# Row sums of a causal attention: partial sums of probability tiles made by adding DMAs in place of GpSimd additions, and a new layout of these tiles

## The reference

```python
q = (x @ wq).reshape(4, 512, 32, 32)
k = (x @ wk).reshape(4, 512, 8, 32)         # each key head serves 4 query heads
v = (x @ wv).reshape(4, 512, 8, 32)
q, k = rope(q), rope(k)
scores = q . k / sqrt(32), causal
attn = softmax(scores)                      # here: exp(score - row max) / row sum
x = layernorm(x + (attn @ v) @ wo)
hidden = silu(x @ (gate_t * gate_s).T) * (x @ (up_t * up_s).T)   # 3584 wide
out = layernorm(x + hidden @ (down_t * down_s).T)
```

## Time and profile before

| | us |
|---|---|
| median of 2 runs | 1869.38 (1867.28 to 1871.48) |
| the profiled execution, its time | 1868.12 |
| its span in the trace | 1866.4 |
| PE busy in it | 1807.0 (97%) |
| DVE, ACT, POOL busy in it | 1187.7, 710.5, 543.6 |

### The profile page before, as it was taken

One profiled execution on the slowest core, in us unless ns is written; L12 is line 12 of the kernel. 1 busy time (PEld: TensorE's weight loads), 2 busy tenths in 40 slices (PEclk: granted clock), 3 DMA queues, 4 the chain that ended last, 5 costly groups with the idle time before them and its releaser, 6 DMA issues.

```text
span 1866.4 us, 27364 instructions
## 1 busy us (share of the span) xinstructions
PE 1807.0 (97%) x10528; PEld 882.0 (47%) x10528; DVE 1187.7 (64%) x2047; ACT 710.5 (38%) x1112; POOL 543.6 (29%) x845
## 2 busy tenths in 40 slices
PE   7889999999999998999999999999999999999997
PEld 4545655555555543444444444444444444444443
DVE  7877778668768764445544444745656765667645
ACT  5443444444434444436433343342232322222221
POOL 1354546456546564131000000211321211112103
PEclk9999999999999999999999999999999999999999
DMA  8543234334334398557644353649321211232301
GB/s 246 118 103 78 54 85 125 83 80 116 90 52 114 81 212 221 209 208 263 236 171 150 107 195 126 215 148 211 127 66 53 79 66 51 72 104 85 107 12 79
DMA packets 228162, 233.13 MB, mean 125 GB/s; under 512 B 183872, under 2 KB 184128, under 8 KB 228032
## 3 DMA queue, kind: packets, MB, share of 16 engines
q1 hardware_dynamic: 227168, 230.99, 42.2%
q10 hardware_dynamic: 864, 0.39, 0.1%
HBM read 122.55 MB, written 72.88 MB: 105 GB/s over the span
## 4 chain that ended last, share of the span: by engine, by line
PE 85%; DVE 6%; issue 3%; SPq 2%; POOL 2%; ACT 1%; DMA 1%; ACTq 0%; DVEq 0%; POOLq 0%
PE bank L1053 31%; PE bank L948 20%; PE bank L1074 13%; PE bank L1087 6%; PE bank L998 4%; PE bank L960 3%; PE bank L984 3%; PE bank L1013 2%; SPq L1587 2%; DVE down_forms L1391 1%; PE bank L963 1%; DVE gate_blocks L1385 1%; POOL p_tiles L1451 1%; DVE row_max L1267 0%; DVE up_blocks L1375 0%
## 5 line engine op out<-in xcount | busy, mean ns | idle before, releaser
L1053 PE MATMUL bank<-x_forms,weight_forms 128*128 128x512 f16 x3136 | 700.9, 379 | 12.7 <-DVE gate_blocks L1375 4.4
L1053 PEld LDWEIGHTS bank<-x_forms,weight_forms 128*128 128x128 f16 x3136 | 305.3, 98 | 387.0 <-DVE gate_blocks L1375 7.1
L1139 ACT ACTIVATE p_tiles<-bank 128x512 f32<-128x512 f32 (+1 forms) x352 | 193.0, 556 | 276.6 <-PE bank L984 273.5
L1267 DVE TENSOR_REDUCE row_max<-bank 128x1 f32<-128x384 f32 (+3 forms) x352 | 220.0, 636 | 98.2 <-PE bank L963 96.6
L1074 PE MATMUL bank<-down_forms 128*128 128x512 f16 x1152 | 259.6, 381 | 2.4 <-issue 2.4
L948 PE MATMUL bank<-wq_parts,xT_parts 128*128 128x256 f16 x1536 | 219.4, 275 | 8.9 <-DVE wq_parts L1231 8.7
L1410 DVE TENSOR_TENSOR acc<-bank,acc 128x512 f32<-128x512 f32 x188 | 127.6, 687 | 124.2 <-PE bank L1074 64.7
L1443 POOL TENSOR_SCALAR_AFFINE_SELECT p_tiles<-p_tiles 128x128 f32<-128x128 f32 (+2 forms) x352 | 139.0, 403 | 212.2 <-ACT p_tiles L1139 210.9
L1074 PEld LDWEIGHTS bank<-down_forms 128*128 128x128 f16 x1152 | 113.0, 98 | 139.7 <-issue 4.9
L948 PEld LDWEIGHTS bank<-wq_parts,xT_parts 128*128 128x128 f16 x1536 | 144.1, 98 | 56.8 <-issue 14.2
L948 PE MATMUL bank<-wo_parts,att_parts 128*128 128x512 f16 x672 | 170.1, 382 | 0.6 <-DMA att_parts<-att_spill 0.6
(11 more groups left out here) (114 smaller groups left out, 1999.9 us busy)
## 6 DMA issues: line engine op xcount, KB each, us to landing
weight_forms_spill<-weight_forms SPq DMA_DIRECT2D x28, 896.0 KB, 5.7
weight_forms<-weight_forms_spill SPq DMA_DIRECT2D x28, 896.0 KB, 4.5
x_forms_spill<-x_parts SPq DMA_DIRECT2D x56, 256.0 KB, 2.4
w_page<-gateT SPq DMA_DIRECT2D x28, 512.0 KB, 5.0
w_page<-upT SPq DMA_DIRECT2D x28, 512.0 KB, 4.0
w_page<-downT SPq DMA_DIRECT2D x28, 512.0 KB, 4.3
att_spill<-att_made SPq DMA_DIRECT2D x64, 128.0 KB, 2.1
down_forms<-x_spill SPq DMA_DIRECT2D x16, 512.0 KB, 3.4
```

What stands on the lines that cost most here:

```text
L1053: t = nc.tensor.matmul(strassen[bank_set(use)][to][:, :], w_form[:, use % 4, A_FORMS[a_form], k * P:(k + 1) * P], xF[:, :, B_FORMS[b_form] ...
L1139: nc.scalar.activation(p32[j][:, h0:h0 + heads, :], bank[5 + m % 2][:, 0:heads * n].rearrange("p (h c) -> p h c", c=n), ACT.Exp, scale=SCO ...
L1267: nc.vector.tensor_reduce(mx[:, u % 2, i, h0:h0 + ROW_HEADS[i]], bank[3 + m % 2][:, 0:ROW_HEADS[i] * n].rearrange("p (h c) -> p h c", c=n) ...
```

## The change

- `presum` is gone. In its place stands `fold`: a DMA issued by POOL that adds (`accum_op`) tile j + 1 into the queries that tile j shares with it, for j = 2, 1 and 0. Each fold waits for the `pv` of tile j and, for j < 2, until the fold before it has landed. These waits are on POOL, which runs in order.
- `sums` of the groups 0 to 28 takes tile 0 alone, since fold 0 has put everything into it. Groups 29 and 30 take two tiles and have the folds 2 and 1; the last one takes all four, as before.
- The next group's `exp` of tile j waits for the landing of fold j - 1 (j = 1, 2, 3), or for `sums` (j = 0).
- A tile is laid out by blocks of 128 queries, then heads, in place of heads, then queries. So what a fold adds is one contiguous run on each partition: 1536, 1024 and 512 numbers for folds 0, 1 and 2, or 768, 512 and 256 KB in all.
- The planner's figures: 1.2 us of POOL for a fold, 5.0 us until it lands, `sums` 7 ranks behind the last key scores in place of 3.5.

```diff
+EARLY = NU * UG - 3
+FOLD_ISSUE, FOLD_LANDS = 1.2, 5.0
+def summed(q):
+    return 1 if q < EARLY else 2 if q < NU * UG - 1 else NT
@@
-        freed = [("pv", *last, j), ("sums", *last) if j < 2 else ("presum", *last, j - 1)] if q else []
+        freed = [("pv", *last, j), ("sums", *last) if j < summed(q - 1) else ("fold", *last, j - 1)] if q else []
@@
-        if j in (1, 2) and not final:
-            put(PO, at + 4, .2 + REP * (S - (j + 1) * P) / 410, "presum", u, G, j,
-                after=[("pv", u, G, j)] + [("presum", u, G, 2)] * (j == 1))
+        if j < NT - 1 and j + 1 >= summed(q):
+            put(PO, at + 3.5, FOLD_ISSUE, "fold", u, G, j, after=[("pv", u, G, j)] + [("fold", u, G, j + 1)] * (j < NT - 2), lands=FOLD_LANDS)
@@
-        put(PE, at + 3.5, 3.0 if final else 1.5, "sums", u, G, takes="T", after=[("causal", *one)] + [("presum", u, G, 1)] * (not final))
+        put(PE, at + (7 if q < EARLY else 3.5), (.9, 1.6, 2.2, 2.5)[summed(q) - 1], "sums", u, G, takes="T", after=[("causal", *one)] + (
+            [("fold", u, G, summed(q) - 1)] if not final else []))
@@
-        p32 = [p_all[:, p_starts[j]:p_starts[j + 1]].rearrange("p (h c) -> p h c", h=REP) for j in range(NT)]
+        p32 = [p_all[:, p_starts[j]:p_starts[j + 1]].rearrange("p (i h c) -> p i h c", h=REP, c=P) for j in range(NT)]
@@ matmuls of pv and sums
-  value, p32[j][:, h, :]
+  value, p32[j][:, :, h, :]
@@ sums, on PE
-                    tiles = 2
-                    if u * UG + G == NU * UG - 1:
-                        tiles = NT
-                    else:
-                        on.wait_ge(s_pre, 2 * (u * UG + G + 1))
+                    q = u * UG + G
+                    tiles = summed(q)
+                    if tiles < NT:
+                        on.wait_ge(s_fold[tiles - 1], 16 * (q + 1))
@@ exp, on ACT
-                    if j < 2:
+                    if j < summed(q - 1):
                         on.wait_ge(s_sums, q)
                     else:
-                        on.wait_ge(s_pre, 2 * q - (j - 2))
-                    nc.scalar.activation(p32[j][:, h0:h0 + heads, :], bank[5 + m % 2][:, 0:heads * n].rearrange(
-                        "p (h c) -> p h c", c=n), ACT.Exp, scale=SCORE_DOWN).then_inc(s_exp, 1)
+                        on.wait_ge(s_fold[j - 1], 16 * q)
+                    nc.scalar.activation(p32[j][:, :, h0:h0 + heads, :], bank[5 + m % 2][:, 0:heads * n].rearrange(
+                        "p (h i c) -> p i h c", h=heads, c=P), ACT.Exp, scale=SCORE_DOWN).then_inc(s_exp, 1)
@@ on POOL
-                elif kind == "presum":
+                elif kind == "fold":
                     u, G, j = which
                     q = u * UG + G
                     on.wait_ge(s_pv, NT * q + NT - j)
-                    on.wait_ge(s_pre, 2 * q + 2 - j)
-                    to = p32[j][:, :, P:S - j * P]
-                    nc.gpsimd.tensor_tensor(to, to, p32[j + 1][:, :, :], ALU.add).then_inc(s_pre, 1)
+                    if j < NT - 2:
+                        on.wait_ge(s_fold[j + 1], 16 * (q + 1))
+                    to, more = (t.rearrange("p i h c -> p (i h c)") for t in (p32[j][:, 1:NT - j, :, :], p32[j + 1][:, :, :, :]))
+                    e.dma_start(to, more, accum_op=ALU.add).then_inc(s_fold[j], 16)
```

More of the change, by code:

```diff
@@ L729, in block_kernel @@
         s_sk, s_exp, s_caus, s_pv = sem("score_k"), sem("exp"), sem("causal"), sem("pv")
-        s_pre, s_sums = sem("presum"), sem("sums")
+        s_fold, s_sums = [sem(f"fold_dma{j}") for j in range(NT - 1)], sem("sums")
         s_scale_att, s_ahi, s_alo = sem("att_scaled"), sem("att_hi"), sem("att_lo")
@@ L879, in attention_over @@
             on.wait_ge(s_exp, NU * NKEY)
-            on.wait_ge(s_pre, 2 * (NU * UG - 1))
+            for j in range(NT - 1):
+                on.wait_ge(s_fold[j], 16 * len([q for q in range(NU * UG) if j + 1 >= summed(q)]))
             on.wait_ge(s_sums, NU * UG)
@@ L997, in tensor_program @@
                     for h in range(REP):
-                        t = nc.tensor.matmul(bank[PV_BANK[q]][h * HD:(h + 1) * HD, lo:S], value, p32[j][:, h, :],
+                        t = nc.tensor.matmul(bank[PV_BANK[q]][h * HD:(h + 1) * HD, lo:S], value, p32[j][:, :, h, :],
                                              start=j == NT - 1, stop=j == 0, tile_position=(0, h * HD),
@@ L1005, in tensor_program @@
                     trans_free((kind, *which))
-                    tiles = 2
-                    if u * UG + G == NU * UG - 1:
-                        tiles = NT
-                    else:
-                        on.wait_ge(s_pre, 2 * (u * UG + G + 1))
+                    q = u * UG + G
+                    tiles = summed(q)
+                    if tiles < NT:
+                        on.wait_ge(s_fold[tiles - 1], 16 * (q + 1))
                     for j in range(tiles):
                         for h in range(REP):
-                            t = nc.tensor.matmul(bank[TRANS][h * HD:(h + 1) * HD, j * P:S], ones[:, :], p32[j][:, h, :],
+                            t = nc.tensor.matmul(bank[TRANS][h * HD:(h + 1) * HD, j * P:S], ones[:, :], p32[j][:, :, h, :],
                                                  start=j == 0, stop=j == tiles - 1, tile_position=(0, h * HD))
@@ L1440, in gpsimd_program @@
                     m = key_n(*which)
-                    block = p32[j][:, h0:h0 + KEY_HEADS[j], 0:P]
+                    block = p32[j][:, 0, h0:h0 + KEY_HEADS[j], :]
                     on.wait_ge(s_exp, m + 1)
```

## The result

| | us |
|---|---|
| median before, 2 runs | 1869.38 (1867.28 to 1871.48) |
| median after, 2 runs | 1998.7 (1992.45 to 2004.95) |
| ratio | 1.069, 95% interval 1.054 to 1.085 |
| the profiled execution after, its time and span | 2004.95, 2003.2 |

The change makes the kernel 7% slower: 129 us, where the prediction had 27, and above its range. The profiled execution is the slower of the two, by 12.5 us.

What follows compares the result with a forecast made beforehand. The prediction took PE as the bound, busy 1807.0 of 1866.4 us. Saving 19 us of `sums` against 46 us of new waits for fold landings gave +27 us, 1895 us; range 1850 to 1950 us.

Steps and rivals of the forecast that it cites:

- F = 15.1 us: Time from the end of tile 2's `pv` to fold 0's landing, three landings in a row; bounds 8.5 to 21.3 us.
- the nine windows: Nine groups with 12.5 to 13.4 us of PE work between tile 2's `pv` and `sums`; waits of 21.6 us in total.
- the six shorter ones: Six groups with less PE work before `sums`, 7.7 to 11.5 us; waits of 24.6 us in total.
- the fourteen: Fourteen groups with 15.9 to 21.1 us of PE work before `sums`; no waits for the folds, 0 us.
- The prices of an adding DMA: Two documented rules for fold landings: three take 9.6 us by the queue formula, 13.2 us if adding halves the rate.
- Waits at `sums`, 46 us: PE's new waits for the landing of fold 0, summed over all 29 groups: 46 us.
- POOL's queue ... isn't counted twice: `causal` behind a waiting fold on POOL can delay the last `pv` 1 us, time otherwise waited at `sums`; nothing added.
- the last sign that the prediction gave: A wait at `pv` for `causal` longer than at `sums` would make POOL's queue, not fold 0's landing, the price.
- Other transfers ... is in the bounds of F: Folds' 47 MB beside other DMAs: a fold takes longer during a 512 KB load, covered by bounds 8.5 to 21.3 us.
- That "behind it" costs nothing more: Next group's projections, scores, `pv` and `exp` stand behind the landing waits; only PE's waits at `sums` were priced.
- 19 us, all on the bound: Dropping the 384-column matmuls of `sums` saves PE 0.65 us in each of 29 groups, 19 us.
- the chain of landings sets every group: Rival: three landings take 18 us or more, +83 us, 1951 us; chance 0.37 for anything above 15.9 us.

Runs made afterwards that it cites:

- dma_small_folds: Changed kernel with each of the three folds cut to 64 KB, leaving out nearly all of the additions, same order and waits; 1888.1 us, ratio 1.012.
- dma_copy_folds: Changed kernel with each fold copying the same bytes instead of adding them, softmax of nearly 0 for all scores; 1896.5 us, ratio 1.015.
- After_plain_stack: Changed kernel with SyncE's transposing DMAs made plain ones of the same bytes, softmax of nearly 0 for all scores; 1977.9 us, ratio 1.059.
- layout_only: Kernel before with only the new layout of the probabilities: two additions on POOL, sums over two tiles, old order; 1868.2 us, ratio 1.000.

## Why the prediction was wrong

Its direction, slower than before, was right; its size was not, 27 us for 129. By its steps:

- **F = 15.1 us** is the step that failed first. The estimate fits the three median landings (15.5 us) and group 14 (15.4), but group 14 is the shortest of the 29. Measured in every group, F is 17.4 us in the nine windows and 19.9 in the six shorter ones. Each F has 1.4 us or more ahead of its three issues, and the landings have a tail that a median hides: fold 1 took up to 8.1 us, fold 0 up to 15.7. The waits at `pv` and `sums` were 32.5 us in the nine for a forecast of 21.6, 46.1 in the six for 24.6, and 5.1 in the fourteen for 0: 84 for 46. The prediction's own sum with 17.4 and 19.9 gives 42 + 53 - 19 = +76 us.
- **The prices of an adding DMA.** The Trainium skill's page "Collectives: The Full Stack" (The bandwidth ceiling) says of the adding step of a collective that it reads two sources and runs at half the rate of a copy. The trace agrees for the engines' time: 13.1% of 2003 us against 6.8% of 1894 us is a factor of 2.0 for the same bytes. In time to land it was a factor of 1.3 to 1.7. The formula of the Trainium skill's page "DMA: Bandwidth & Descriptors" (Anatomy of one DMA) gives 2.6, 3.2 and 3.8 us, by estimate; the copies took 2.9, 3.8 and 3.9, the adding ones 3.9, 5.1 and 6.5.
- **Waits at `sums`, 46 us**: measured 44.3, and that is luck. The 46 stood for all of PE's waits in the windows, and as much again came at `pv`.
- **"POOL's queue ... isn't counted twice"** was right for after: PE waited 42.2 us at `pv` for `causal`, and nearly all of it inside F, so that `sums` would have waited otherwise. It fails where F is shorter than the window: in dma_small_folds 23 us, and in dma_copy_folds 10 us, of the waits at `pv` come on top of what `sums` would have waited. There fold 2 and fold 1 stand side by side in POOL's queue with the `causal` of tile 0 behind both. By the last sign that the prediction gave, a wait at `pv` longer than at `sums`, these two runs have POOL's queue as the price; after, with 42.2 and 44.3, does not.
- **"Other transfers ... is in the bounds of F"**: part of the price is in the tail of F, and part lies elsewhere, 21.2 us of PE's waits for `q_stack`, which the sum has no term for. After_plain_stack still has 12.8 us of them.
- **That "behind it" costs nothing more**: the prediction named `exp` behind the folds, but priced PE's waits only at `sums`. ACT waited 173.4 us for folds, and PE 8.7 us for `exp`, 7.5 for `max_rows` at the `sums` moved past it.
- **The clock has no term in the sum.** Each us that PE waited was counted as one us. The granted clock fell from 0.99 to 0.93 over the stretch, in which PE idled 17% of the time in place of 3%, and the same matmuls took 40 us longer. That it fell because PE idles is the reading that the table above supports (0.99 with 16 to 18 us idle, 0.98 with 25 to 30, 0.96 or 0.97 with 39 to 66 and in one case 94, 0.93 with 97 to 129), and the 12 longest waits with their stretches at 1.2 GHz, but no run changed the one without the other. Nor are the 40 us all loss: the work in the six short windows took 71 us for 57 forecast, in part by the clock, and by so much PE waited less for the landings.
- **"19 us, all on the bound"**: the work is gone, as small folds show (busy 611.1 us for 620.5), but half of it went back through the clock, and the idle time of every version with three additions is larger than before.
- **The slope, 15 us for each us of F**: between dma_copy_folds and after it was 21, as the clock and the waits for `q_stack` go with it.
- **The layout and presum, 0**: right (layout_only, 0.9996).

The rival "the chain of landings sets every group", with F of 18 us or more, +83 us and 1951 us, had the reason, and came nearer to the waits: 102 us, against 77 measured at `pv` and `sums` and 46 forecast. It too lacked the waits for `q_stack`, `max_rows` and `exp` (34 us) and the 40 us of slower matmuls, without which 77 - 19 = 58 of the 132 us stay. What stays open: why the landings have this tail, and how much of the loss is the landing itself, how much the load of adding DMAs on the other transfers and how much the new order.

## What to carry to other kernels

For a chain of transfers take the mean with its tail and the gaps between them, not the sum of medians, and measure it in more than one group: the group worked out in detail here was the mildest of 29. A transfer that waits for a transfer holds its whole queue: price what stands behind it on that engine by itself, wherever the chain is shorter than the window. When PE is the bound and runs at its high clock, look for slower matmuls beside every new wait: here 111 us of idle time came with 40 us of them, though no run shows the one without the other. And work taken off the bound is worth nothing if the order around it leaves its time as new waits; here 14 to 19 us of matmuls went, and none of the ten kernels that left them out was faster than before.
